# Window attention with GroupNorm on one core: the bias of V moved from TensorE to GpSimd, the turn of the maxima moved, TensorE's loop lengthened, scale and shift made in six steps

## The reference

```python
g = v.reshape(B_, G, C_ // G, H_, W_)                     # G = 32
m, s = mean(g, (2, 3, 4)), var(g, (2, 3, 4));  xn = (g - m) / sqrt(s + eps)
xs = roll(xn, (-SHIFT, -SHIFT), axis=(-2, -1))
qkv = einsum('bchw,oc->bohw', xs, w_qkv) + b_qkv          # 384 x 128 weights
scores = einsum('bxyhqd,bxyhkd->bxyhqk', q, k) / sqrt(hd) # 49 x 49 for a head and window
attn = softmax(scores); out = einsum('bxyhqk,bxyhkd->bxyhqd', attn, v)
x + roll(out, (SHIFT, SHIFT), axis=(-2, -1))
```

## Time and profile before

| | us |
|---|---|
| median of 3 runs (lowest, highest) | 965.36 (963.44, 965.49) |
| the profiled execution, its own time | 963.83 |
| its span, from the first to the last instruction | 962.0 |
| PE busy, share of the span | 897.0, 93% |
| DVE, ACT, POOL busy | 737.9, 655.8, 596.9 |
| mean granted TensorE clock | 0.981 of full speed |

### The profile page before, as it was taken

How to read it: one execution, slowest core, us unless ns; L and a number is a source line. 1 busy time by engine, 2 the same in 40 slices (tenths; PEclk the granted TensorE clock), 3 DMA queues, 4 the chain that set the end, 5 groups by cost and what they waited for, 6 DMA issues and landing times.

```text
span 962.0 us, 104413 instructions
## 1 busy us (share of the span) xinstructions
PE 897.0 (93%) x46595; PEld 723.9 (75%) x46595; DVE 737.9 (77%) x1404; ACT 655.8 (68%) x1297; POOL 596.9 (62%) x1067
## 2 busy tenths in 40 slices
PE   0489999999999999999999999999999999999984
PEld 0367888887788888887788888888778888888863
DVE  8567878787887878788887878787877777777752
ACT  2356777777677777777677777777667777777652
POOL 1436666665666666666666666666666666666641
PEclk9979999999999999999999999999999999999996
DMA  9402112211211221122121000000000000000001
GB/s 371 173 4 67 50 50 67 67 49 51 67 50 50 67 67 46 54 67 67 34 67 50 29 21 33 33 26 24 34 27 24 33 33 26 24 33 33 24 29 37
DMA packets 29920, 51.96 MB, mean 54 GB/s; under 512 B 3650, under 2 KB 28868, under 8 KB 29764
## 3 DMA queue, kind: packets, MB, share of 16 engines
q1 hardware_dynamic: 29892, 51.59, 15.2%
HBM read 25.89 MB, written 25.69 MB: 54 GB/s over the span
## 4 chain that ended last, share of the span: by engine, by line
PE 87%; DVE 7%; issue 3%; POOL 1%; DMA 1%; ACT 1%; SPq 0%; POOLq 0%; DVEq 0%; ACTq 0%
PE psum L737 17%; PE psum L789 12%; PE psum L757 11%; PE psum L775 10%; PE psum L721 8%; PE psum L709 8%; PE psum L702 8%; PE psum L801 4%; PE psum L764 4%; PE psum L717 3%; PE psum L744 2%; DVE neg_max L576 2%; DVE stats L496 2%; DVE q_halves L561 1%; DMA image<-in_x_dram 1%
## 5 line engine op out<-in xcount | busy, mean ns | idle before, releaser
L374 ACT ACTIVATE probs_t<-psum,exp_scale 128x800 f32<-128x800 f32 x256 | 223.2, 923 | 179.6 <-PE psum L764 179.6
L576 DVE TENSOR_REDUCE neg_max<-psum 100x16 f32<-100x784 f32 x256 | 249.4, 974 | 44.7 <-PE psum L737 19.9
L293 POOL TENSOR_SCALAR neg_halves<-neg_max 100x32 bf16<-100x32 f32 x128 | 60.4, 472 | 290.3 <-DVE neg_max L576 290.3
L737 PEld LDWEIGHTS psum<-k_hi,q_masks 32*128 32x128 f16 x8192 | 175.6, 91 | 47.6 <-issue 46.4
L737 PE MATMUL psum<-k_hi,q_masks 32*128 32x49 f16 x8192 | 198.4, 179 | 4.5 <-issue 2.5
L737 PE MATMUL psum<-k_lo,q_masks 32*128 32x49 f16 x4096 | 182.9, 179 | 0.0
L737 PEld LDWEIGHTS psum<-k_lo,q_masks 32*128 32x128 f16 x4096 | 161.2, 91 | 0.0
L306 POOL TENSOR_TENSOR stage<-mixed,image 128x343 f32 (+7 forms) x256 | 144.2, 582 | 10.2 <-DVE mixed L601 6.8
L351 ACT ACTIVATE xn<-image,shift_c,rstd_c 128x21 f32 (+6 forms) x256 | 131.9, 572 | 8.7 <-DVE shift_c L556 6.9
L757 PE MATMUL psum<-q_masks,k_hi 32*64 32x100 f16 x8192 | 129.5, 220 | 6.4 <-issue 3.8
L789 PE MATMUL psum<-probs_t,v_rows 64*32 64x100 f32 x8192 | 131.8, 253 | 1.2 <-issue 1.2
(11 more groups left out here) (120 smaller groups left out, 1865.4 us busy)
## 6 DMA issues: line engine op xcount, KB each, us to landing
out_dram<-stage SPq DMA_DIRECT2D x64, 224.0 KB, 2.1
out_dram<-stage SPq DMA_DIRECT2D x64, 168.0 KB, 1.9
image<-in_x_dram SPq DMA_DIRECT2D x32, 224.0 KB, 2.6
image<-in_x_dram SPq DMA_DIRECT2D x1, 6104.0 KB, 27.2
image<-in_x_dram SPq DMA_DIRECT2D x34, 168.0 KB, 2.5
image<-in_x_dram SPq DMA_DIRECT2D x6, 896.0 KB, 9.7
image<-in_x_dram SPq DMA_DIRECT2D x1, 728.0 KB, 14.2
w_nat<-in_L_conv_w_qkv_dram SPq DMA_DIRECT2D x1, 192.0 KB, 2.5
```

The lines of the kernel that those rows point to most:

```text
L374: nc.scalar.activation(probs_t[:, 2 * u:2 * u + 2, :, :].rearrange("p h a q -> p h (a q)"), psum[:, COL_BANKS[u], 0:PAIRS * ROWS2], ACT.Ex ...
L576: nc.vector.tensor_reduce(neg_max[:, par, 2 * j:2 * j + 2, :], psum[0:ROWS2, ROW_BANKS, 0:GT] .rearrange("p h (w k) -> p h w k", k=TOK), A ...
L737: last = nc.tensor.matmul(psum[:, ROW_BANKS.start + h - 2 * j, w * TOK:(w + 1) * TOK], q_masks[rows, par, low + w * ROWS2:low + w * ROWS2 ...
```

## The change

1. **Bias of V.** The matmul L717 is gone, with its tables, its two small DMAs and what DVE did to prepare them. The first of the three products of V now starts the sum. The rows of attention sum to one, so the bias is added to `mixed` instead: POOL gets `add_bias`, one in-place float32 instruction per group at the head of its step, and `add_image` waits for it.
2. **Turn next to the spread.** PE's `turn_max` stands behind row scores 0 and directly ahead of `spread_inverse`, and writes into bank 5. So it waits until V of the step is evacuated, V waits for the evacuation of the maxima, `scale_rows` waits for it too, and the evacuation waits for the spread. On ACT it moves behind Q. Row scores 0 no longer wait for it.
3. **PE's loop** runs to step 127, so that steps 128 and 129 alone stand behind it. In step 127 it makes a Q and a K of a group 128 that does not exist; two semaphores are raised by hand for that.
4. **Scale and shift** are kept twice, by image parity, so `offer` need not wait for the old image's end. The work is cut into six steps, with pieces behind the masks (`ahead`) and ahead of the join (`between`).
5. **Statistics.** A chunk of the next image stands behind the masks and ahead of the inverse. For the first image's turn five chunks lie in step 0 and three in step 1, instead of three each in steps 2 and 3; DVE waits for the whole second image before step 0.

```diff
+            def add_bias(g, half):
+                pool.wait_ge(mixed_done, g + 2)
+                pool.sem_inc(waited, 1)
+                nc.gpsimd.tensor_scalar(mixed[:, half, :, :], mixed[:, half, :, :], bias[:, 2:3], None, ALU.add).then_inc(bias_added, 1)
+
             def add_image(g, t, half):
-                pool.wait_ge(mixed_done, g + 2)
+                pool.wait_ge(bias_added, g + 1)
...
             def step(g, n, par):
+                if live(g - 3):
+                    add_bias(g - 3, 1 - par)
                 if live(g - 1):
                     split_max(g - 1, 1 - par)
...
             def evac_neg(g):
                 act.wait_ge(neg_mm, g + 1)
+                wait(act, inv_mm, g)
                 wait(act, col_mm, g)
...
             def offer(b):
-                wait(dve, xn_ready, b * 2 * BANDS)
-                scatter_groups()
+                wait(dve, xn_ready, (b - 1) * 2 * BANDS)
+                nc.vector.transpose(mean_c[:, :], mean_row[:, :])
+                link(nc.vector.transpose(rstd_c[:, b % 2, :], var_row[:, :]))
...
             def scale_rows(g, par):
                 dve.wait_ge(inv_mm, g + 1)
+                dve.wait_ge(neg_ready, min(g + 2, GROUPS) if isinstance(g, int) else g + 2)
...
             def change_image(b):
+                g = (b * BANDS - 4) * 2
+                for ahead, between in ((None, lambda: gather_channels(b)),
+                                       (turn_channels, group_mean),
+                                       (group_variance, guess_root),
+                                       (lambda: refine_root(1), lambda: refine_root(1)),
+                                       (lambda: refine_root(NEWTON - 2), scatter_groups),
+                                       (None, lambda: offer(b))):
+                    step(g, g // 2, g & 1, ahead=ahead, between=between)
+                    g += 1
...
             def project_v(g, par):
                 wait(pe, v_evac, g)
                 wait(pe, mixed_done, g - 1)
-                nc.tensor.matmul(psum[:, V_BANK, :].rearrange("p (a d) -> p a d", a=PAIRS), ones_rows[:, :, :].rearrange("p s k -> p (s k)"),
-                                 bias_rows[:, None, :].broadcast_to([C, PAIRS, C]), start=True, stop=False, skip_group_check=True)
+                wait(pe, neg_ready, g - 1)
...
             def turn_max(g, after_v=True):
+                if after_v:
+                    pe.wait_ge(v_evac, g + 2)
+                else:
+                    pe.wait_ge(mixed_done, g)
                 pe.wait_ge(neg_split, g + 1)
...
             def step(g, par):
...
                 if live(g - 2):
                     sum_keys(g - 2)
-                if live(g - 1):
-                    turn_max(g - 1)
                 if live(g - 2):
                     weigh(g - 2, par)
...
                     row_scores(g, par, 0)
+                if live(g - 1):
+                    turn_max(g - 1, live(g))
                 if live(g - 2):
-                    spread_inverse(g - 2, live(g))
+                    spread_inverse(g - 2)
...
-            with pe.Fori(1, GROUPS // 2 - 1) as n:
+            with pe.Fori(1, GROUPS // 2) as n:
                 step(2 * n, 0)
                 step(2 * n + 1, 1)
-            for g in range(GROUPS - 2, GROUPS + 2):
+            for g in range(GROUPS, GROUPS + 2):
                 step(g, g & 1)
```

128 lines of the change are left out of this document (55 added, 73 removed).

## The result

The changed kernel takes 942.52 us (median of 4 runs, 941.08 to 942.85), the kernel before beside it 965.38 us. The ratio is 0.9764, 95% interval 0.9750 to 0.9778. The profiled execution took 941.08 us, span 938.9. The forecast was 920.8 us, range 909 to 934: the sign was right, but of the 43.0 us forecast 22.8 came, and the time lies above the range.

What follows compares the result with a forecast made beforehand. PE, busy 93% of the span, was taken as the bound. Gains of 24.8 (steady step), 8.5 (changes of image), 2.0 (start) and 7.7 (end) sum to 43.0 us: 963.83 - 43.0 = 920.8 us, range 909 to 934.

Steps and rivals of the forecast that it cites:

- The steady step: Groups 5 to 126: step falls from 6.885 to 6.68 us, set by the exponentials; gain 24.8 us over 121 steps.
- PE stays the bound: Rival on the steady step: sums start within 0.02 us of the exponentials' end, step 6.57, 907.4 us; chance 0.15.
- the turn gains nothing: Rival on the steady step: the moved turn still needs its own change of shape, step 6.78, 932.8 us; chance 0.22.
- The end: From V of group 126 on: the longer PE loop avoids "issue" waits (stands) of written-out code; gain 7.7 us, ends 5 and 9.
- The changes of image: Three changes within groups 5 to 126: new places for small instructions save 8.5 of 9.5 us, ends 6 and 9.5.
- POOL: `add_bias` on POOL: taken as 0.53 us and hidden in idle time, cost nothing, but the next bound.
- that rival: POOL becomes the bound: `add_bias` at 1.84 us delays the split of K, 1001 us; against the change from 1.54; chance 0.03.
- The start: Groups 0 to 5: no bias matmul and no chunks in step 2; gain 2.0 us, ends 1 and 3.
- its edits doing nothing: Rival at the changes of image: another piece of DVE's chain is late, no gain there, 929 us; chance 0.05.

Runs made afterwards that it cites:

- e13: Kernel before with only the turn moved next to the spread, with its bank, waits and evacuation on ACT; ratio 0.9880.
- e10: Kernel before with only PE's loop run to the last group; 955.01 us, ratio 0.9895.
- e14: Changed kernel with no scale and shift pieces at the three changes of image, so later images are normalised with wrong numbers; 926.23 us, ratio 0.9600.
- e9: Kernel before with only scale and shift kept twice and made in six steps, and the statistics moved with them; ratio 1.0011.
- e4: Changed kernel with all scale and shift pieces behind `mixed` and the bias of V left out altogether; 935.61 us, ratio 0.9687.
- e2: Changed kernel with the bias of V left out altogether; 937.09 us, ratio 0.9697.
- e3: Changed kernel with every scale and shift piece behind `mixed`, ahead of maximum 1; 940.17 us, ratio 0.9729.
- e6: Changed kernel with the second image's first statistics in steps 2 and 3, four chunks each, instead of steps 0 and 1; 940.49 us, ratio 0.9745.
- e11: Changed kernel with the bias of V added on ACT and POOL's image addition in its old place, one step later; 944.12 us.
- e7: Changed kernel with the bias of V added on ACT and POOL's image addition moved behind the split of x; 950.75 us.

## Why the prediction was right or wrong

**The steady step: right.** 6.68 forecast, 6.692 measured. The loop over the exponentials binds, as worked out: in the step read before, ACT's two exponentials and then PE's sums are

```profile
484.43 1.74 ACT L373 ACTIVATE probs_t<-psum,exp_scale 128x800 f32<-128x800 f32 x2 [0.95 <-PE psum L772]
```

```profile
486.32 0.91 PE L783 MATMUL psum<-probs_t,sum_rows 128*32 128x49 f32 x64
...
489.43 0.22 PE L752 MATMUL psum<-ident,neg_halves 100*128 100x100 bf16 x1
489.48 0.29 PE L808 MATMUL psum<-inv_rows,pick_head 128*128 128x49 f16 x5
```

The exponentials end at 486.17 and the sums start at 486.32: hand-over 0.15, forecast 0.13. The turn stands 0.05 us ahead of the spread, as taken, and moved alone (e13) it gave 0.109 us, forecast 0.10. The bias alone gave 0.087 us and not its 0.215, since the rest is the wait for the exponentials. The rivals "PE stays the bound" and "the turn gains nothing" are out, the second by e13 directly.

**The end: right**, 7.7 us, and by the forecast mechanism: from V of group 126 to the sums of that group (905.96 to 920.23) 14.3 us pass, forecast 14.1. Two details were off and nearly cancel: no stand remains, where I left 1.0 us, and the bias addition lies open for 1.26 us, not 0.53. The longer loop alone (e10) took 8.5 us off the end. The Trainium skill (Runtime: NRT & Kernel Launch, section Instruction fetch mechanics) says that a taken branch breaks the sequential prefetch when its target lies outside the two pages held, and that kernels therefore prefer full unrolling where possible. For these passes of PE the runs decide against unrolling. What the four stands waited for no view shows.

**The changes of image: the step that failed** is the term of 8.5 us. I wrote "In the new order the pieces are three or four small instructions each and stand where a chunk of the statistics stood or where DVE waits for the sums", and left 0.3 us for each change. A change costs some 5.2 us (all three 15.7 by e14), and the new places gained nothing over the old: alone, in e9, the kernel got no faster. Three errors lie in that sentence. I read the waits of the earlier trace rows as a fault of one place; but where the pieces now stand 0.43 and 0.31 us are free in a step (e14), behind `mixed` 0.34 (e4), the pieces last 5.4 us a change undisturbed, and DVE is in the chain from the sums to the maxima, K and the column scores. I gave the pieces no price of their own, and none for POOL's work beside them. And half of them stand not where DVE waits for the sums, but between the inverse and the join, where POOL worked without a break in the rows shown.

**POOL: wrong in price, right in the main.** "The nearest row is the tensor by scalar of the same size, 0.53 us" was the row of a conversion to float16. In float32 it is 1.26 us, between my far row (0.92) and the point of 1.54 us at which that rival decides. In the steady step it is hidden: without it (e2) the step is 6.69 us as well. At the changes, where I named no work beside it, it costs 2.5 to 4.8 us: it stretches DVE's instructions, the pieces where they stand behind `mixed` (e3), the masks and the low inverse in the changed kernel, and in those steps DVE is on the path.

**The start: wrong.** 2.0 forecast, -0.7 measured to V of group 5. The wait for the second image, "0.5 us at most", was 2.25 us: the instruction ahead of the masks of step 0 comes 1.2 us earlier than before (32.97 against 34.13), and the masks wait for the transfer until 35.86. In e6, without that wait and the five chunks there, the fourth `mixed` comes only 0.1 us earlier, so this is not the cause, which stays open.

**The range** was too narrow because I bounded the gain at the changes of image by 6 and 9.5 us and gave 0.05 to its edits doing nothing. A loss had no case, although DVE stands at 77% busy in the earlier trace rows, and adding up its small pieces in the trace of before would have shown over 5 us for each change.

## What to carry to other kernels

An engine that is idle for a fifth of each step, but in five short waits (DVE in e14: 0.43, 0.30, 0.31, 0.08 and 0.20 us of 6.69), has no room for work that outlasts one of them. Count what is free in each place, not in the step. The cheapest test is to leave the extra work out and see whether the bound is worth the effort. A price read beside an idle neighbour holds only there: ask which instruction of GpSimd will run beside a VectorE instruction in its new place, and the other way round. Where the last passes of a loop were written out and PE stands without a releaser in them, try them in the loop.

## What was not expected of the hardware

- DVE and POOL hold each other up. DVE instructions on 8 to 32 columns that have two inputs from SBUF, or are a tensor by scalar, last 0.15 to 0.19 us beside an idle POOL and up to 0.99 us beside a running one (e11). The stretched ones mostly end within 0.05 us of POOL's instruction. Reductions, copies and transposes of these sizes stay at 0.21 us or less in all runs, and those that read PSUM (`summed`, `mixed`, the maxima) keep their 0.63, 0.56 and 0.97 us. The Trainium skill (GPSIMD Engine Reference, section Key points) says that GpSimd shares its SBUF interfaces with VectorE, with contention for DVE instructions in a 2-port perf mode or with two SBUF inputs. For two inputs the traces agree; the mode of the tensor by scalar no trace shows.
- When it happens is not settled. Beside one and the same bias addition (L291 in e3) two-input instructions took 0.19 us (L519, L521) and 0.51 (L539), and DVE's tensor by scalar 0.17 (L531) and 0.47 (L527).
- It goes both ways: POOL's image addition in three pieces lasts 1.28 us in one place (e11) and 2.41 us beside DVE's maximum and masks (e7). There its piece of 28 columns takes 1.38 us and ends at 495.99, 0.1 us behind the masks; in the changed kernel such a piece takes 0.24 us.
- POOL's tensor by scalar on 128x392 takes 1.26 us from float32 to float32 and 0.53 us from float32 to float16.
- PE's waits at row scores 0 carry "issue" in e3 (12.0 us), with VectorE's maximum and POOL's splits late in just those steps. All but one of them end 0.1 us behind POOL's split of K. A row with "issue" can thus be a wait for another engine, and the view of waits does not tell.
